# Gate of the token stage: gate weights stationary in four column groups, partial sums joined by a selector matmul

## What is computed

```python
x = x + _L0_xattn_ref(_layernorm(x), ctx, ctx, Wq, Wk, Wv, Wfc, bfc)
h = _layernorm(x).reshape(-1, 512)
logits = h @ gate_weight.T                      # (2048, 8): the gate
scores = softmax(logits)
topk_w, topk_i = _group_limited_topk(scores)    # 4 groups of 2, best 2 groups, best 2 experts
routed = sum over the chosen experts of topk_w * (silu(h @ g.T) * (h @ u.T)) @ d.T
shared = silu(h @ sh_gate.T) * (h @ sh_up.T) @ sh_down.T
out = x + routed + shared
```

## Time and profile before

| what | value |
|---|---|
| median of 3 runs | 788.76 us |
| lowest and highest run | 786.3 and 791.9 us |
| the profiled execution | 787.48 us |
| its span, first to last instruction | 785.7 us |
| mean granted clock of TensorE | 0.996 |
| PE busy | 758.3 us, 97% of the span |
| ACT busy, DVE busy | 441.4 us (56%), 568.4 us (72%) |
| L1427, the gate, all 64 matmuls in 128 records | 15.3 us busy on PE |
| token stage | about 296 to 388 us of the span |

### The profile page before, as it was taken

The page is one execution under the profiler, slowest core; times in us unless marked ns, Lnnn a source line. Parts: engine busy times, 40 slices in busy tenths (PEclk is TensorE's granted clock), DMA queues, the critical chain, the costliest instruction groups (busy, mean ns, idle before and its releaser), DMA issues.

```text
span 785.7 us, 15967 instructions
## 1 busy us (share of the span) xinstructions
PE 758.3 (97%) x5151; PEld 406.0 (52%) x5152; DVE 568.4 (72%) x1194; ACT 441.4 (56%) x859; POOL 268.7 (34%) x224
## 2 busy tenths in 40 slices
PE   6998989999999989999999999999999999999997
PEld 4553533333433324666655565555555555555553
DVE  5767779999999966887589886555555555546667
ACT  3666579999999984777634553433434343332231
POOL 3362008999994301666200101111111111024431
PEclk9999989999999999999999999999999999999999
DMA  8998746656645799997588466777767777569995
GB/s 329 348 396 244 247 140 215 181 171 192 196 120 173 230 344 324 330 408 245 172 242 228 121 156 156 177 183 173 186 174 176 177 176 175 129 163 291 282 239 155
DMA packets 161784, 172.09 MB, mean 219 GB/s; under 512 B 103680, under 2 KB 117504, under 8 KB 161216
## 3 DMA queue, kind: packets, MB, share of 16 engines
q1 hardware_dynamic: 150012, 128.89, 56.6%
q0 software_dynamic: 11120, 41.43, 16.7%
q10 hardware_dynamic: 596, 1.07, 0.4%
HBM read 105.40 MB, written 42.73 MB: 189 GB/s over the span
## 4 chain that ended last, share of the span: by engine, by line
PE 82%; DVE 7%; DMA 5%; ACT 3%; issue 2%; SPq 1%; DVEq 0%; ACTq 0%
PE psum L1473 29%; PE psum L1485 15%; PE psum L1322 8%; PE psum L1409 7%; PE psum L1308 6%; PE psum L1236 4%; PE psum L1212 4%; PE psum L1339 2%; DMA sb_weights<-in_wdn 2%; DMA sb_hT<-sb_h 2%; PE psum L1427 1%; PE psum L1188 1%; PE psum L1418 1%; PE psum L1401 1%; DVE sb_weights L1755 1%
## 5 line engine op out<-in xcount | busy, mean ns | idle before, releaser
L1473 PE MATMUL psum<-sb_weights,sb_rows 128*128 (+1 forms) x1608 | 250.8, 313 | 0.1
L1473 PEld LDWEIGHTS psum<-sb_weights,sb_rows 128*128 128x128 f16 x1608 | 157.2, 98 | 91.4 <-DMA sb_rows<-xnT_dram 0.5
L1024 ACT ACTIVATE sb_weights<-psum,sb_rows 128x512 f32<-128x512 f32 x256 | 158.3, 684 | 16.8 <-PE psum L1308 15.0
L1705 DVE TENSOR_REDUCE sb_rows<-psum 128x4 f32<-128x1024 f32 x128 | 149.9, 1214 | 5.6 <-PE psum L1236 5.6
L1485 PE MATMUL psum<-sb_weights,sb_hT 128*128 (+1 forms) x630 | 147.4, 379 | 3.4 <-DMA sb_hT<-sb_h 3.4
L893 POOL DMA_INDIRECT sb_rows<-xn_rows,sb_slot_tok x39 | 38.4, 984 | 217.8 <-DVE sb_rows L2295 147.8
L1485 PEld LDWEIGHTS psum<-sb_weights,sb_hT 128*128 128x128 f16 x630 | 61.3, 98 | 69.0 <-DMA sb_hT<-sb_h 4.6
L1101 ACT ACTIVATE psum<-psum 128x352 f32<-128x352 f32 x71 | 31.8, 448 | 113.3 <-DVE psum L1956 113.2
L1308 PE MATMUL psum<-sb_weights 50*128 50x512 f16 x256 | 90.1, 391 | 3.0 <-ACT sb_weights L1024 2.6
L1322 PE MATMUL psum<-sb_weights 128*32 128x256 f32 x1024 | 82.9, 396 | 0.0
L1236 PE MATMUL psum<-sb_weights 48*128 48x256 f16 x512 | 73.3, 275 | 0.6 <-DVE sb_rows L1705 0.6
(11 more groups left out here) (267 smaller groups left out, 1016.7 us busy)
## 6 DMA issues: line engine op xcount, KB each, us to landing
sb_weights<-in_wgu SPq DMA_DIRECT2D x20, 704.0 KB, 7.7
sb_weights<-in_wgu POOLq DMA_DIRECT2D x20, 704.0 KB, 5.6
sb_weights<-in_wdn SPq DMA_DIRECT2D x17, 768.0 KB, 6.2
slot_y<-sb_rows SPq DMA_DIRECT2D x39, 256.0 KB, 2.3
sb_weights<-q_parts SPq DMA_DIRECT2D x96, 64.0 KB, 2.3
x_dram<-sb_rows SPq DMA_DIRECT2D x24, 256.0 KB, 4.1
q_parts<-sb_weights SPq DMA_DIRECT2D x16, 256.0 KB, 4.5
sb_rows<-in_x POOLq DMA_DIRECT2D x16, 256.0 KB, 4.5
```

The costliest lines, as they stand in the source:

```text
L1024: nc.scalar.activation(probs[G % 2][:, kt, pair * 512:(pair + 1) * 512], bank[4 + f % 2], ACT.Exp, scale=exp_scale[:, n:n + 1]).then_inc(e ...
L1473: mm = nc.tensor.matmul(bank[GU_BANKS[par][which]][:, 0:F], x_T[:, xp * D + k * P:xp * D + (k + 1) * P], gu(wp, k, which), start=(k == 0 a ...
L1705: nc.vector.tensor_reduce(to[:, :, j // UB, :, j % UB, qt], psum[:, banks[qt] * 512:(banks[qt] + 2) * 512] .rearrange("p (a h k) -> p a h ...
```

## The change

The gate is computed with the operands exchanged. The gate weights (128x8) are now stationary and the transposed rows (128x128) move. The four pieces k of the contraction go to four column groups of the array and leave four partial sums in partitions 32k to 32k + 7 of `bank[6 + s][:, 0:128]`, experts in partitions and tokens along the columns. ACT copies this 128x128 block to SBUF (`gate_copy`). A second f32 matmul (`gate_total`) takes the copy as stationary operand and a 128x8 selector `gate_sum` as moving one, which adds the four partial sums and turns the result to tokens in partitions; `gate_out` copies it as before.

`gate_total(t - 4)` stands behind `gate(t - 3)` on PE, one turn later than the gate it belongs to, and `gate_out` moves one turn back too. The selector is made once by a DVE reduction over the identity at the kernel's start. Since partitions that no group writes are read by the copy, PE clears both banks once by multiplying zeros (`gate_clear`). The wait for 15 copied logits ahead of `early_up(0, 0, 0, 1)` goes away, and the last `gate_total` stands behind `early_up(1, 1, 0, 0)`. `ln2_shift` moves into unused words of another tile.

```diff
@@ constants and buffers
+        gate_sum = sb("gate_sum", [P, NE])
-        ln2_shift = sb("ln2_shift", [P, 2])
+        ln2_shift = mv[:, 2, :]
+        gate_rows = [words(KV_0 + 2 * HALF + s * P, P) for s in range(2)]
@@ ACT
+            def gate_copy(t, s):
+                act.wait_ge(gate_parts, t + 1)
+                nc.scalar.copy(gate_rows[s], bank[6 + s][:, 0:P]).then_inc(gate_copied, 1)
             def gate_out(t, s):
                 act.wait_ge(gate_ready, t + 1)
-                nc.scalar.copy(logits[:, bass.ds(t, 1), :], bank[6 + s][:, 0:NE].unsqueeze(1)).then_inc(gate_evac, 1)
+                nc.scalar.copy(logits[:, bass.ds(t, 1), :], bank[6 + s][:, P:P + NE].unsqueeze(1)).then_inc(gate_evac, 1)
@@ ACT, loop over t
                 if t >= 3:
-                    gate_out(t - 3, (t - 3) % 2)
+                    gate_copy(t - 3, (t - 3) % 2)
+                if t >= 4:
+                    gate_out(t - 4, t % 2)
@@ ACT, behind the loop
-            gate_out(TILES - 3, 1)
+            gate_copy(TILES - 3, 1)
+            gate_out(TILES - 4, 0)
             lnt_out(TILES - 2, 0, TILES // 2 - 1)
             silu(0, 0, 0, shared_inv(0))
-            gate_out(TILES - 2, 0)
+            gate_copy(TILES - 2, 0)
+            gate_out(TILES - 3, 1)
             square(0, 0)
             hidden_high(0, 0)
             lnt_out(TILES - 1, 1, TILES // 2 - 1)
             silu(1, 1, 0, shared_inv(1))
-            gate_out(TILES - 1, 1)
+            gate_copy(TILES - 1, 1)
+            gate_out(TILES - 2, 0)
             square(1, 1)
             hidden_high(1, 1)
+            gate_out(TILES - 1, 1)
@@ PE
             def gate(t, s):
                 pe.wait_ge(lnt_evac, t + 1)
                 if not (isinstance(t, int) and t < 2):
                     pe.wait_ge(gate_evac, t - 1)
                 for k in range(KD):
-                    mm = nc.tensor.matmul(bank[6 + s][:, 0:NE], lnT[s][:, k * P:(k + 1) * P], gw_sb[:, k, :],
-                                          start=(k == 0), stop=(k == KD - 1))
-                mm.then_inc(gate_ready, 1)
+                    mm = nc.tensor.matmul(bank[6 + s][VW * k:VW * k + NE, 0:P], gw_sb[:, k, :], lnT[s][:, k * P:(k + 1) * P],
+                                          start=True, stop=True, tile_position=(0, VW * k))
+                mm.then_inc(gate_parts, 1)
+            def gate_total(t, s):
+                pe.wait_ge(gate_copied, t + 1)
+                nc.tensor.matmul(bank[6 + s][:, P:P + NE], gate_rows[s], gate_sum[:], start=True, stop=True).then_inc(gate_ready, 1)
+            def gate_clear(s):
+                nc.tensor.matmul(bank[6 + s][:, 0:P], zero_row[:, 0:P], zero_row[:, 0:P], start=True, stop=True)
+            pe.wait_ge(gate_sums, 1)
+            for s in range(2):
+                gate_clear(s)
             ot_transpose(0, 0, 0)
@@ PE, in both loops over t, behind gate(t - 3, ...)
+                gate_total(t - 4, t % 2)
@@ PE, behind the loop
             gate(TILES - 3, 1)
+            gate_total(TILES - 4, 0)
             ln_transpose(TILES - 2, 0)
             early_up(0, 0, 0, 0)
             gate(TILES - 2, 0)
+            gate_total(TILES - 3, 1)
             pe.wait_ge(x2_done, TILES)
             ln_transpose(TILES - 1, 1)
-            pe.wait_ge(gate_evac, TILES - 1)
             early_up(0, 0, 0, 1)
             gate(TILES - 1, 1)
+            gate_total(TILES - 2, 0)
             early_up(1, 1, 0, 0)
+            gate_total(TILES - 1, 1)
@@ DVE, ahead of norm_block(0)
+            dve.wait_ge(consts, 2)
+            nc.vector.tensor_reduce(gate_sum[:], ident[:].rearrange("p (k e) -> p e k", k=KD)[:, 0:NE, :], AX.X,
+                                    ALU.add).then_inc(gate_sums, 1)
```

More of the change, by code:

```diff
@@ L263, in build @@
         lnT = [row(6), row(7)]
+        gate_rows = [words(KV_0 + 2 * HALF + s * P, P) for s in range(2)]
+        assert KV_0 + 2 * HALF + 2 * P <= P3_0
         xb_sb = lnT
@@ L359, in build @@
         lnt_ready, lnt_evac, gate_ready, gate_evac = sem("lnt_ready"), sem("lnt_evac"), sem("gate_ready"), sem("gate_evac")
+        gate_parts, gate_copied, gate_sums = sem("gate_parts"), sem("gate_copied"), sem("gate_sums")
         x2_stored = [sem(f"x2_stored{s}") for s in range(2)]
@@ L1456, in _ @@
                     gate(i * TPB + (r - 3), (r + 1) % 2)
+                    gate_total(i * TPB + (r - 4), r % 2)
             for t in range(TILES - TPB, TILES):
```

## The result

| | before | after |
|---|---|---|
| median, 4 runs each | 787.53 us | 795.34 us |
| lowest and highest run | 782.8, 791.9 | 792.3, 798.8 |
| profiled execution | 787.48 us | 795.89 us |
| its span | 785.7 us | 794.1 us |
| its mean granted clock | 0.996 | 0.991 |

The ratio after to before is 1.0116, 95% interval 1.0086 to 1.0147: the kernel became slower by 6.8 to 11.6 us. The medians lie 7.8 us apart. The prediction had +3.8 us (0.48%) and 0.89 on "within 1%". The time is inside its range of 788 to 796 and the direction is that of its sum, but the size is more than double.

A forecast was written before the change was run, and what follows sets the result against it. PE and a loop ACT to DVE to ACT to PE were taken as nearly level limits. Terms +0.8 (clear 0.47, loop 0.35), +1.18, -0.40, -0.14, +2.36 gave +3.8: 791.3 us, 792 on the median, range 788 to 796.

The forecast's parts named there:

- The gate on PE: Token stage: gate with total falls from 0.84 to 0.74 us a tile, 1.6 us saved if PE alone limited.
- rival C: Token stage: the four column groups don't overlap, 0.56 us a tile more, 797 us; chance 0.07.
- rival B: Token stage: groups fully parallel, form changes free, loop not binding; gate costs a quarter, -2.1 us, 785.4; chance 0.05.
- The loop: Token stage, ACT to DVE to ACT to PE: gate_copy delays it, +0.35 us over the stage instead of -1.6.
- Rival A: Token stage: the loop has slack and hides the copy; stage wins 1.6 us, total 789.3; chance 0.12.
- gate_clear: Ahead of the first attention transpose: two f32 clearing matmuls on PE that nothing covers, +0.47 us.
- The stall ahead of gate(13): Stage end: PE waits for tile 11's logits, copied in ACT's turn 15; first shared expert +1.18 us later.
- The last total: Routing: gate_total(15) stands behind a whole shared expert unit, so the exp comes 2.36 us later.
- All 3.8 us arrive at PE: From exp to sel DVE is almost gapless and PE already waits, so the whole delay reaches PE.
- Rival D: Near the end: late routing is absorbed by shorter DMA stalls or DVE gaps; +0.5 to +1.5, about 788.5; chance 0.10.
- The sum: Whole kernel: 787.48 + 3.8 = 791.3 us profiled, 792 said for the median; chance 0.66.
- The chances: Whole kernel, against a 1% (7.9 us) threshold: faster 0.02, same 0.89, slower 0.09.

The follow-up runs named there:

- copy8: Changed kernel with gate_copy cut from 128x128 to 128x8, logits wrong; ratio to the kernel before 1.0076.
- copy_first: Changed kernel with gate_copy and gate_out ahead of the square root in every ACT turn; ratio to the kernel before 1.0047.
- all_three: Changed kernel with both gate copies ahead of the square root every turn, gate_total(15) ahead of early_up(1, 1, 0, 0), no gate_clear; ratio to the kernel before 1.0020.
- stall_only: Kernel before, old gate, with PE made to wait for tile 12's logits ahead of gate(13); ratio to the kernel before 1.0045.
- early_total: Changed kernel with gate_total(15) ahead of early_up(1, 1, 0, 0) and its gate_out ahead of square(1, 1); ratio to the kernel before 1.0044.
- late_logits: Kernel before with the last gate behind early_up(1, 1, 0, 0) and its copy behind hidden_high(1, 1); ratio to the kernel before 1.0023.
- after_again: The changed kernel itself, unaltered, profiled and timed once more; ratio to the kernel before 1.0086.
- The padded kernel: Kernel before with 18 tiny f32 matmuls, result not used, at PE's start while it waits for input; ratio to the kernel before 1.0054.

## Why the prediction was right, and where it failed

**The gate on PE: right.** 0.84 to 0.74 us a tile was forecast; the chain shows 0.34 + 0.32 + 0.49 for gate, total and transposes against 0.79 + 0.49, which is 0.13 less. The groups overlap (rival C is out), and their gain is far from a quarter's (rival B is out).

**The loop: right in kind, half in size.** Forecast +0.35 us over the stage in place of -1.6, measured +0.67. copy8 shows that 0.5 of it is the copy's width. Rival A, slack in the loop, is out. The working took ACT's share as all there is; copy_first and all_three showed that with the copy off the path DVE's `second_part` still holds the loop, so that 0.37 us of the 1.6 that PE alone would save come through, and the rest would be lost with a free copy too.

**gate_clear: right**, 0.54 for 0.47, all of it on the path.

**The stall ahead of gate(13): right in place and length, wrong in what follows it.** Forecast +1.18, measured +1.29, by the copy in ACT's turn 15 behind the square root that was named. The step that failed is the one after it: "Between that and the next expert unit there is ... 4.75 instead of 5.15". It costed the unit behind the stall at its old 3.58 us, as if idle time left TensorE as it was. 4.72 came only where the clock held; in the five profiles of the new gate in which it fell it was 5.82 to 6.39, and stall_only has 6.54 for the old gate's 5.15. The term that was left out is 1.4 to 1.7 us in these profiles, as much as the stall; it is the largest miss of the sum that a trace shows, and it does not account for the whole.

**The last total: right**, 2.48 for 2.36, and the order alone gives it back (early_total) or brings it about in the old kernel (late_logits).

**"All 3.8 us arrive at PE": right.** Exponential to `sel` is 12.24 us in every profile, and PE's wait ahead of L1567 grew from 0.70 to 2.1. Rival D, absorption, is out; nothing behind gives time back.

**The sum.** The steps as forecast gave +3.8; without a fall of the clock they measure +4.4, so their sizes account for 0.6. The fall adds 1.7 in the profiled execution and 1.4 to 1.7 in five of the seven others with the stall. These make 6.1 us there, and about 5.6 on average if six executions in eight have a fall, which the timed runs do not confirm. The medians are 7.8 apart and after_again's mean 7.5. The 1 to 2 us left, more if the fall is rarer than in the profiles, are in no step, and their cause is open. The padded kernel shows that an edit outside the path can move the time by 4.2 us, of which its profile shows 2.6 as waits behind SP's long issues.

**The chances.** 0.89 on "within 1%" was too sure. The range went to 796, and 1% over the median was 796.6; the terms that were known badly, the loop's share (up to 0.9) and what follows PE's idling, could add far more than they could take off.

## What to carry to other kernels

Before a step is put one turn later, follow the semaphore that it raises to the loop's last turn, for there the later place can be behind something that the loop never waited for: here both costs, 1.3 and 2.4 us, arose where the loop ends, and the gain, 0.1 us a tile, in it. When PE and a loop over ACT and DVE are level, a shorter tile on PE is worth little (here nothing, and 0.37 of 1.6 us with the copy moved), and what is added to the other engines' loop is paid for. Charge a stall of TensorE with the lower clock that can follow it. Before one profile's number is laid to an edit, find the tile where it arises: one late transfer hid half of what copy_first had won. And compare changes of half a per cent with a kernel that has only been padded.

## What the runs showed of the hardware beside this

- After 1.6 to 1.8 us without a matmul, in a stretch where TensorE had otherwise not stood for over 0.4 us, the next unit began at the lower clock in 6 of 8 profiles (0.57 and 0.55 in the windows shown) and ran at 1.00 in two.
- A form with 8 stationary columns in four column groups and 128 moving ones: eight f32 passes in 0.34 us (0.043 each), where a pass of the old gate, with 128 stationary columns and 8 moving ones, took 0.79/8 = 0.10.
- The issue of one transfer on SP's queue took 0.57 us in most profiles and 1.24 at the same place in another; that of a transposing one 1.22 and 2.54.
- 18 matmuls of 8 columns in idle time at the kernel's start went with +0.54% (0.26 to 0.82) of the time. In both kernels that had them an issue on SP's queue took 1.3 to 2.0 us instead of 0.42 in nearly every turn of a loop that runs 120 us and more later, and PE stood 2.6 and 4.1 us for it.
